# Ten filter units and most loads of the first spectra placed in the last turns of the first stage; ScalarE's relu of the convolution branch placed earlier in its turn

## The reference, cut to what matters

```python
h = maximum(layernorm(x), 0)                      # layer 0
x = x + relu(norm_adj @ h @ W.T + b)              # norm_adj from adj + eye
h = maximum(layernorm(x), 0)                      # layer 1, x is now x2
c = relu(bn1(conv1(h)))                           # 1x1 convolution
x_conv = relu(bn2(conv2(c)) + h)                  # 17 taps along the nodes
s = h @ w_se.T + b_se
A = exp(-(|s_n|^2 + |s_m|^2 - 2 s_n.s_m)) * adj
x_nmp = A @ relu(h @ w_msg.T + b_msg)
x = x + gru([x_conv, x_nmp], h)                   # r, z, n gates
```

## Time and profile before

| | |
|---|---|
| time, median of 3 runs | 1805.54 us (1805.25 to 1806.76) |
| the profiled execution | 1806.71 us, of which its span is 1804.9 us |
| PE busy | 1770.6 us, 98% of the span |
| DVE, ACT, POOL busy | 1213.0, 997.1, 836.5 us |
| chain that ended last | PE 94%, DVE 2%, issue 2%, POOL 1%, ACT 1% |

### The profile page before, as it was taken

One profiled execution on the slowest core, in us unless ns is written; L12 is line 12 of the kernel. 1 busy time (PEld: TensorE's weight loads), 2 busy tenths in 40 slices (PEclk: granted clock), 3 DMA queues, 4 the chain that ended last, 5 costly groups with the idle time before them and its releaser, 6 DMA issues.

```text
span 1804.9 us, 29811 instructions
## 1 busy us (share of the span) xinstructions
PE 1770.6 (98%) x10214; PEld 1568.7 (87%) x10214; DVE 1213.0 (67%) x2306; ACT 997.1 (55%) x1781; POOL 836.5 (46%) x989
## 2 busy tenths in 40 slices
PE   6999999999999989999999999999999999999998
PEld 5999999999999979999988888888888888888887
DVE  7999999999999825555784544544544545545545
ACT  4888888888888866656542332332332332333322
POOL 5788888887777527656731221221221212212211
PEclk9999999999999999999999999999999999999999
DMA  6566566665555446676973435345345344344442
GB/s 205 173 197 221 197 212 206 201 221 189 200 193 189 153 132 147 166 174 158 226 202 101 85 102 121 81 103 123 78 107 118 77 113 104 87 117 89 101 110 42
DMA packets 513876, 262.56 MB, mean 145 GB/s; under 512 B 365639, under 2 KB 473543, under 8 KB 513726
## 3 DMA queue, kind: packets, MB, share of 16 engines
q1 hardware_dynamic: 513182, 260.58, 52.8%
q10 hardware_dynamic: 544, 0.07, 0.0%
HBM read 151.51 MB, written 109.05 MB: 144 GB/s over the span
## 4 chain that ended last, share of the span: by engine, by line
PE 94%; DVE 2%; issue 2%; POOL 1%; ACT 1%; DMA 0%; SPq 0%; ACTq 0%; DVEq 0%; POOLq 0%
PE P L113 70%; PE P L585 6%; PE P L912 5%; PE P L614 4%; PE P L654 4%; PE P L767 3%; PE P L633 1%; PE P L594 1%; DVE yo L792 0%; DVE wsum L730 0%; POOL axl L550 0%; DMA col<-in_cols 0%; DVE wh0l L742 0%; POOL af L547 0%; DMA yt<-y_d 0%
## 5 line engine op out<-in xcount | busy, mean ns | idle before, releaser
L894 POOL TENSOR_TENSOR xnx1l<-xnf,xnx1h 128x1024 fp32r<-128x1024 f32 x16 | 44.0, 2749 | 336.7 <-ACT xnx1h L887 336.7
L894 POOL TENSOR_TENSOR xnx0l<-xnf,xnx0h 128x1024 fp32r<-128x1024 f32 x15 | 41.6, 2772 | 317.7 <-ACT xnx0h L887 317.7
L1011 ACT ACTIVATE tr<-P,cold 128x512 f32<-128x512 f32 x64 | 44.2, 690 | 194.4 <-PE P L113 194.4
L1014 ACT ACTIVATE nn<-gn,col 128x512 f32<-128x512 f32 x64 | 46.4, 725 | 179.3 <-DVE gn L1035 179.3
L1044 DVE SCALAR_TENSOR_TENSOR tz<-tz,tr 128x512 f32<-128x512 f32 x63 | 43.6, 693 | 145.3 <-ACT tz L1025 145.2
L585 PE MATMUL P<-ah,hd 128*128 128x256 f32 x512 | 123.0, 383 | 12.2 <-ACT hd L383 12.2
L1025 ACT ACTIVATE tz<-P,cold 128x512 f32<-128x512 f32 x63 | 43.4, 689 | 159.6 <-PE P L113 159.6
L547 POOL TENSOR_TENSOR af<-af,at 128x512 f32<-128x512 f32 x64 | 111.0, 1735 | 42.1 <-ACT af L345 40.2
L1031 DVE SCALAR_TENSOR_TENSOR gn<-tr,gn 128x512 f32<-128x512 f32 x64 | 44.9, 701 | 127.3 <-ACT tr L1011 127.3
L550 POOL TENSOR_TENSOR axl<-af,axh 128x512 fp32r<-128x512 f32 x64 | 101.8, 1591 | 55.3 <-ACT axh L363 55.3
L585 PEld LDWEIGHTS P<-ah,hd 128*128 128x128 f32 x512 | 93.8, 192 | 22.7 <-ACT hd L383 12.2
(11 more groups left out here) (200 smaller groups left out, 6402.1 us busy)
## 6 DMA issues: line engine op xcount, KB each, us to landing
xh_d<-xst SPq DMA_DIRECT2D x64, 320.0 KB, 4.5
xl<-xh_d SPq DMA_DIRECT2D x40, 512.0 KB, 6.3
y_d<-yo SPq DMA_DIRECT2D x80, 256.0 KB, 2.5
x<-in_x SPq DMA_DIRECT2D x64, 256.0 KB, 2.7
a<-in_adj SPq DMA_DIRECT2D x64, 256.0 KB, 3.0
at<-in_adjt SPq DMA_DIRECT2D x64, 256.0 KB, 4.2
x_d<-x SPq DMA_DIRECT2D x64, 256.0 KB, 4.5
xn_d<-xt SPq DMA_DIRECT2D x64, 256.0 KB, 4.3
```

The costliest lines, as they stand in the source:

```text
L894: e.e.tensor_tensor(o[1][:, :, :], xnf[p % 2][:, :, :, :].rearrange("p c i t -> p c (i t)"), o[0][:, :, :], ALU.subtract).then_inc(done, 1)
```

## The change

Four things are done.

1. **Units.** Units 0 to 9 move from behind the first stage into its last turns, in front of the distances (`UNITS_INSIDE`) or at the end of a turn (`UNITS_BEHIND`). The first six use one PSUM bank (AG), the next four use four. DVE copies these ten out, counted by the new semaphore `wevd`; ACT copies the rest. Behind the stage 16 units remain before the first bin.
2. **Loads.** The tiles `x`, `a`, `eye2` and `at` of the first stage are placed where `xl` lies later, so that `xl` is free as soon as they are. Blocks 0 and 1 are loaded in two parts: groups 0 to 14 in turn NB+4, group 15 in turn NB+8. The four stores of a group are put in another order (both chunks of the lower half of the bins first, then the upper half) with semaphores `sxa`, `sxb` for the halves, and stand at the start of SP's turn.
3. **Relu.** ACT's relu that makes `h1` moves from behind the second `xst` copy to right behind `msh`, in every turn.
4. ACT waits for the first stage before its 22nd copy (unit 21), not its 23rd.

```diff
@@ first_sync
+            if live(i, 11, NB):
+                g, c, r = (i - 11) // 4, (i - 11) % 2, (i - 11) % 4 // 2
+                e.wait_ge(S[f"xe{c}"], 4 * g + 4)
+                e.e.dma_start(xh_d[g][:, c, 16 * r * NF:16 * (r + 1) * NF],
...
-            if live(i, 11, NB):
-                g, c, r = (i - 11) // 4, (i - 11) % 4 // 2, (i - 11) % 2 * NF
@@ first_scalar
+            if live(i, 6):
+                b = i - 6
+                e.wait_ge(S["tcm0"], b + 1)
+                e.wait_ge(S["tcm1"], b + 1)
+                e.wait_ge(S["dft1"], b - 1)
+                e.e.activation(h1[b % 2][:, :, :], tcm[:, :, 0:256], ACT.Relu).then_inc(S["h1"], 1)
@@ first_vector
+            for n in UNITS_BEHIND.get(i - 1, ()):
+                unit_out(e, n)
...
+            for n in UNITS_INSIDE.get(i, ()):
+                unit_out(e, n)
@@ first_tensor
+            for n in UNITS_INSIDE.get(i, ()):
+                filter_unit(e, n)
...
+            for n in UNITS_BEHIND.get(i, ()):
+                filter_unit(e, n)
@@ filter_unit, unit_out
+        ONE_BANK, EARLY = 6, 10
+        UNITS_INSIDE = {NB + 3: (1,), NB + 4: (3,), NB + 5: (5,)}
+        UNITS_BEHIND = {NB + 2: (0,), NB + 3: (2,), NB + 4: (4,), NB + 5: (6, 7, 8, 9)}
+        def unit_bank(n):
+            return AG if n < ONE_BANK else 4 + n % 4
...
+            if n < ONE_BANK:
+                e.wait_ge(S["aglo"], NB)
+                e.wait_ge(S["wevd"], n)
+            else:
+                for name in ("aglo", "uvf", "xxlo", "tcm0", "tcm1"):
+                    e.wait_ge(S[name], NB)
+                units_out(e, max(n - 3, ONE_BANK))
...
+            if n < EARLY:
+                e.e.tensor_copy(dst, src).then_inc(S["wevd"], 1)
+            else:
+                e.e.copy(dst, src).then_inc(S["wev"], 1)
@@ loads
+        def load_first_spectra(e):
+            for name in ("x2", "hd", "deg0", "ah"):
+                e.wait_ge(S[name], NB)
+            e.wait_ge(S["sxa0"], 32 * (NG // 2))
+            e.wait_ge(S["sxa1"], 32 * (NG // 2 - 1))
+            for q in range(2):
+                load_groups(e, q, 0, NG - 1)
+        def load_last_spectra(e):
+            e.wait_ge(S["sxa1"], 32 * (NG // 2))
+            for q in range(2):
+                load_groups(e, q, NG - 1, NG)
@@ sync
+                if i == NB + 4:
+                    load_first_spectra(e)
+                if i == NB + 8:
+                    load_last_spectra(e)
             first_stage_done(e)
-            for q in range(2):
-                load_spectra(e, q)
@@ scalar
-            for n in range(UNITS):
-                if n == UNITS - 4:
+            for n in range(EARLY, UNITS):
+                if n == UNITS - 5:
                     first_stage_done(e)
                     spectra_hi(e, 0)
@@ tensor
-            for n in range(UNITS + AHEAD):
+            for n in range(EARLY, UNITS + AHEAD):
                 filter_unit(e, n)
```

More of the change, by code:

```diff
@@ L121 @@
 out0 u x2 sx20 sx21 st1 ag1a ag1 rs1 n1b xn xnt xt sxt xxhi xxlo s uvf uvh uv cm0 cm1 tcm0 tcm1 h1 mshi mslo
-dist af am axhi axlo nmp nm snm dft0 dft1 xe0 xe1 sxh0 sxh1
-unit yz wev lxh0 lxh1 xsum xhi xlo wsum whi wlo frq com mt ye sy0 sy1 sy2 sy3
+dist af am axhi axlo nmp nm snm dft0 dft1 xe0 xe1 sxa0 sxa1 sxb0 sxb1
+unit yz wev wevd lxh0 lxh1 xsum xhi xlo wsum whi wlo frq com mt ye sy0 sy1 sy2 sy3
 lwg0 lwg1 lwg2 lwg3 lwg4 lwg5 wghi wg ly0 ly1 ly2 lxn0 lxn1 lnm0 lnm1 nmhi nmlov nmlop xnhi xnlov xnlop
@@ L195, in gnn_kernel @@
         xx = p1.hl("xx", [128, 512])
+        p1.at = spectra_at = keep.at + 40960
+        xs = [p1(f"x{i}", [128, 2, 256]) for i in range(5)]
+        a_ = [p1(f"a{i}", [128, 2, 256]) for i in range(2)]
+        eye2 = p1("eye2", [128, 512])
+        at = [p1(f"at{i}", [128, 512]) for i in range(7)]
+        x2 = [p1(f"x2{i}", [128, 2, 256]) for i in range(2)]
         stage = Place(nc, p1.at)
@@ L309, in spectrum_out @@
             e.wait_ge(S[f"dft{c}"], b + 1)
-            e.wait_ge(S[f"sxh{g % 2}"], 64 * (g // 2))
+            for half in "ab":
+                e.wait_ge(S[f"sx{half}{g % 2}"], 32 * (g // 2))
             e.e.copy(dst, src).then_inc(S[f"xe{c}"], 1)
@@ L684, in units_in, with load_groups, spectra_loaded @@
             return range(first + n * m // 18, first + n * (m + 1) // 18)
+        def load_groups(e, q, first, end):
+            for c in range(2):
+                e.e.dma_start(xl[q % 2][:, 16 * c + first:16 * c + end, :],
+                              xh_d[first:end, :, c, 64 * q:64 * q + 64].rearrange("g p r -> p g r")).then_inc(
+                                  S[f"lxh{q % 2}"], 16)
+        def load_first_spectra(e):
[9 more added lines that the diff above has]
+                load_groups(e, q, NG - 1, NG)
         def load_spectra(e, q):
-            for n in range(2):
-                e.wait_ge(S[f"sxh{n}"], 64 * (NG // 2))
+            for name in ("sxa0", "sxa1", "sxb0", "sxb1"):
+                e.wait_ge(S[name], 32 * (NG // 2))
             e.wait_ge(S["xhi"], 2 * q - 2)
             e.wait_ge(S["xlo"], 2 * q - 2)
[L692 to L695, removed]
+            load_groups(e, q, 0, NG)
+        def spectra_loaded(e, f):
+            e.wait_ge(S[f"lxh{f // 2 % 2}"], 32 * (f // 4 + 2))
         def bin_of(f):
```

42 lines of the change are left out of this document (14 added, 28 removed).

## The result

The changed kernel takes 1813.78 us (median of 22 executions, 1797.97 to 1815.82), the kernel before 1806.09 us beside it (22 executions, 1805.12 to 1808.62). The ratio is 1.0035, its 95% interval 1.0023 to 1.0048. So it became slower by 0.35%, and the forecast of 1798.9 us was wrong by 14.9 us. The executions do not scatter evenly: two took 1797.97 and 1798.51 us, one 1811.19, and nineteen between 1813.0 and 1815.9. The profiled one took 1813.47 us with a span of 1811.6 us.

A forecast was written before the change was run, and what follows sets the result against it. The first stage's last turns were taken as bound by the chain from `uv` to `nmp`, with PE having room, then by units on PE's path. 7.7 gained less 1.1 for the relu gives 6.6 us: 1805.5 to 1798.9 us, range 1797 to 1801.

The forecast's parts named there:

- Relu, 56 full turns: First stage's full turns: `af` ends 0.53 us later, mostly inside the slack; 0.02 us a turn, 1.1 us lost.
- third rival: Relu lengthens each full turn, 1820 us; or L467 comes first every other turn, 11 us, 1809; chance 0.10.
- Units: First stage's last turns: ten units leave the path ahead of the first bin, 7.15 us, fitting PE's waits almost exactly.
- N: Start of the last `nmp` products at the first stage's end; forecast 660.4 us, 0.4 later than 659.98.
- Clock: PE behind the 3.13 us gap, 661.1 to 665.0 us: with the gap filled, the whole 1.7 us is gained.
- Loads and stores: Handover to second stage: early loads there before 660 us, ACT stalls 1.6 us for stores, first bin at N + 18.2.
- The sum: End of the first stage: first bin at 678.6 us instead of 686.3, 7.7 us gained.
- rival 1: No stall at the stores, no cost in the full turns: gain 8.4 to 9 us, 1796.8 us; chance 0.12.
- Rival 2: Early loads delay `nm_d` on SP, N 1.5 to 2.5 us later: 1801 to 1803 us; chance 0.10.

The follow-up runs named there:

- from turn 20: Changed kernel with the relu at its old place in turns 6 to 19, ahead of `af` from turn 20 on: 1799.54 us, ratio 0.9967.
- turn 7 alone: Changed kernel with the relu at its old place in turn 7 only, early in all other turns: 1798.40 us, ratio 0.9955.
- split last: Changed kernel, relu at its old place, with ACT's wait for the stores and `xh0h` behind the copy of unit 25: 1800.71 us, ratio 0.9971.
- last turns: Changed kernel with the relu behind `msh` only from turn NB+1 on, at its old place before: 1799.49 us, ratio 0.9965.

## Why the prediction was wrong

**The step that failed is "Relu, 56 full turns"**, with 0.02 us a turn booked. It measured 0.27 us a turn, 15 us. The way is the one that my third rival named ("L467 may come first every other turn"), to which I gave 0.10 with the others of its kind; its price of 11 us came from a loss in every other turn alone, and each of the two turns loses. The working of the step was right for a turn that follows a good turn: POOL's multiplication, started behind the reduction, takes 1.28 us (I said 1.3 to 1.4), and the turn stays at 9.83 us. That is shown by 43 and by 55 such turns in the runs "from turn 20" and "turn 7 alone" (turn 20 of the one and turn 8 of the other took 1.40 and 1.41 us), and two executions of the changed kernel itself, at 1798 us, fit it (they have no trace). This size was a right reading and no luck. What I left out: the delay of 0.53 us takes POOL's lead over L475 from 0.67 us to 0.14, and I only asked what happens behind the start, not who starts first. In turn 7, the second in which POOL multiplies, the pipeline is still filling, and the lead was smaller from the outset. I had its row (52.70) and read the duration alone; DVE's row beside it, in the kernel before:

```profile
53.11 1.66 DVE L467 SCALAR_TENSOR_TENSOR x<-x,x 128x512 f32<-128x512 f32 x1
```

53.11 - 52.70 = 0.41 us, less than the delay of 0.53. Turn 7 in the changed kernel, POOL and DVE:

```profile
51.47 2.60 POOL L555 TENSOR_TENSOR af<-af,at 128x512 f32<-128x512 f32 x1 [1.32 <-ACT af L355]
```

```profile
51.50 0.68 DVE L475 SCALAR_TENSOR_TENSOR x<-x,x 128x512 f32<-128x512 f32 x1
```

DVE got through and POOL did not, although its record begins 0.03 us earlier. From there the pairs go on by themselves. The Trainium skill (SBUF — State Buffer, "Who interferes with whom") has it that the order of issue, and not the operation, decides who blocks. Turns A and B agree in that either can be the one that waits: L475 takes 1.67 us behind POOL and 0.68 us ahead of it, POOL's multiplication 1.73 us ahead and 2.61 us behind.

I had also named only one wait (`agl`). In every other turn the wait is for the second `xst` copy; moving that copy took 0.33 us off the pair.

**Units:** right. The ten fit, with 0.60 us for a copy on DVE (2.74 us for four; 0.55 forecast). N moved by 0.68 us with the relu at its old place and by 0.31 with it early, where 0.4 was forecast. **Clock:** right; 1.00 with the gap filled, 0.67 over 5 us with the gap left. **Loads and stores:** right in sum. First bin at N + 18.12 to 18.82 for N + 18.2, `wh0l` 1.74 us for 1.7, stall 1.37 to 2.07 us for 1.6. The sum is 7.2 us in the changed kernel and up to 7.8 in others, and with the relu early the stall makes the difference (2.07 and 1.49 us). My rival 1, a gain of 8.4 us or more without the stall, stays untested: the stall was there in every kernel with ten units and the split at its place, and the run "split last" moved the split, which brings `xh0l` beside `wh0l`. Rival 2 is seen as a wait of ACT for `nm_d` of 0 to 0.47 us; with 0.47 us (run "turn 7 alone") N lies 25.38 us behind the transposes of turn NB+2, with 0.04 us ("last turns") 25.37, so it cost nothing. **The whole without the full turns' loss:** 1798.4 to 1799.5 us in five kernels, for 1798.9 forecast.

What stays open: what in turn 7 tips an execution to one side or the other, why the kernel with the copy moved left the pairs at 350 us, and what fixes the hand-over from turn to turn beyond the rows above. Between the leads of 0.06 us (DVE first) and 0.13 us (POOL first) lie 0.07 us, so anything that moves an engine by that much could; no run isolates it. Of the versions tried the relu behind `af` or at its old place is the one to keep: it beats the kernel before by 7 us and the changed one by 15. The kernel with an exception in turn 7 is as fast, but stands on a lead of 0.14 us.

## What to carry to other kernels

Where two engines lock each other out for an instruction, note not only how long each takes but by how much the one leads the other, and keep that lead above the delay that an edit adds; a slack of the engine behind is not that lead. Check the lead in the turns in which a pipeline fills, too: a steady turn can have two regimes, and the first turns choose. Two groups of times for one kernel, and instructions whose durations alternate from turn to turn, are the signs of it; undoing the edit in a single turn tells it from a cost of each turn.

## What the runs showed of the hardware

- A reduction on DVE with one input does hold up POOL. The multiplication takes 1.28 us beside none; 1.28 us where the reduction overlaps it by 0.21 us (370.53 above); 1.49 where by 0.45 us (360.68); 1.79 where by 0.67 us: the overlap less 0.16 to 0.24 us. In the last two and in turn A it ends 1.04 or 1.05 us behind the reduction's end, as if it began 0.23 us before that end (1.28 - 1.05). The Trainium skill (SBUF — State Buffer, "Who interferes with whom") says that such a reduction never contends; the measurement decides here.
- Who goes first follows the lead sharply. In the thirteen kernels with the reduction at its place and no added wait (turns 7 to 63) DVE's operation went first in 81 turns, all with POOL's record 0.02 to 0.06 us ahead, and POOL in 660, all with 0.13 us or more.
- With the reduction moved the lead alone doesn't tell who goes first. In the kernel before with that edit POOL's record was 0.43 us ahead at 303.05, and it lost and took 2.87 us; at 460.04 it was 0.42 us ahead, and it won and took 1.28 us. DVE's `bn_stats` overlapped its start by 0.51 us both times, so that alone isn't the reason; what differs in the rows is POOL's instruction just ahead (L541 on 119 partitions the first time, on 68 the second). No run isolates that either.
- A semaphore in place of the lock costs 0.25 us more behind the end of the other engine's instruction (0.80 for 0.55 us).
